# Graph network, attention layer: the product for the denominators made 96 columns wide

## The reference, cut to what matters

```python
x_l = (x @ W_l.T + b_l).reshape(n, H, C)
x_r = (x @ W_r.T + b_r).reshape(n, H, C)
z = jax.nn.leaky_relu(x_l[src] + x_r[dst], NEG_SLOPE)
e = jnp.einsum('ehc,hc->eh', z, att)
m = jax.ops.segment_max(e, dst, num_segments=n)
e = jnp.exp(e - m[dst])
denom = jax.ops.segment_sum(e, dst, num_segments=n)
alpha = e / (denom[dst] + 1e-16)
out = jax.ops.segment_sum(alpha[:, :, None] * x_l[src], dst, num_segments=n)
```

## Time and profile before

| | us |
|---|---|
| median of 3 runs | 2270.53 |
| lowest, highest | 2264.11, 2282.12 |
| the profiled execution | 2274.55 |
| its span, first to last instruction | 2272.7 |

### The profile page before, as it was taken

One profiled execution on the slowest core, in us unless ns is written; L12 is line 12 of the kernel. 1 busy time (PEld: TensorE's weight loads), 2 busy tenths in 40 slices (PEclk: granted clock), 3 DMA queues, 4 the chain that ended last, 5 costly groups with the idle time before them and its releaser, 6 DMA issues.

```text
span 2272.7 us, 38002 instructions
## 1 busy us (share of the span) xinstructions
PE 1752.6 (77%) x8603; PEld 1346.9 (59%) x8603; DVE 1805.4 (79%) x5399; ACT 1109.9 (49%) x2822; POOL 858.8 (38%) x861
## 2 busy tenths in 40 slices
PE   2677777898999998734688788778937778777886
PEld 1322224777888787523678678778925555555554
DVE  7988887899899896776877778876287787877775
ACT  0666665887888785200224324233434454444443
POOL 2000000000000000067777777771017777777771
PEclk7665557999999999766566777675557888878778
DMA  4245555765666666055656566552112222222221
GB/s 149 106 147 153 152 151 167 290 232 192 236 254 218 234 249 225 7 169 158 175 162 181 163 171 183 166 167 66 46 37 56 54 55 55 55 55 55 56 55 41
DMA packets 192476, 314.96 MB, mean 139 GB/s; under 512 B 25873, under 2 KB 139416, under 8 KB 182418
## 3 DMA queue, kind: packets, MB, share of 16 engines
q1 hardware_dynamic: 163312, 248.12, 33.4%
q0 software_dynamic: 27712, 63.56, 10.7%
q10 hardware_dynamic: 1250, 0.86, 0.1%
HBM read 232.38 MB, written 80.07 MB: 137 GB/s over the span
## 4 chain that ended last, share of the span: by engine, by line
PE 20%; POOL 17%; DVE 14%; issue 10%; DMA 3%; ACT 2%; SPq 1%; DVEq 1%; POOLq 0%; ACTq 0%
POOL G L683 12%; PE PS L1896 6%; PE PS L1872 3%; POOL G L668 3%; PE PS L2003 2%; PE PS L1897 2%; POOL SCR L668 2%; DVE HOT_R L1159 1%; PE PS L1786 1%; DVE SCR L1334 1%; DMA G<-table,src_idx 1%; DMA G<-table,gather_idx 1%; DMA SCR<-table,src_idx 1%; DVE RX L1349 1%; DVE RX L1594 1%
## 5 line engine op out<-in xcount | busy, mean ns | idle before, releaser
L668 POOL DMA_INDIRECT G<-table,src_idx x252 | 266.1, 1056 | 982.2 <-DMA table<-RX 901.9
L683 POOL DMA_INDIRECT G<-table,gather_idx x415 | 405.4, 977 | 281.0 <-DMA table<-RX 154.8
L2003 PE MATMUL PS<-SCR,OH 128*128 128x256 f32 x830 | 283.9, 507 | 107.9 <-DVE SCR L1631 106.0
L2003 PEld LDWEIGHTS PS<-SCR,OH 128*128 128x128 f32 x830 | 203.8, 255 | 161.8 <-DVE SCR L1631 119.2
L1872 PE MATMUL PS<-RX,OH 128*128 x830 | 189.4, 393 | 122.1 <-DVE SCR L1334 71.5
L1786 PE MATMUL PS<-ALL_R 128*128 128x256 f32 (+3 forms) x2025 | 266.4, 288 | 19.6 <-DVE ALL_R L1222 9.1
L1896 PE MATMUL PS<-AT 128*128 128x128 f32 x830 | 261.9, 412 | 13.5 <-DVE AT L1498 5.9
L1786 PEld LDWEIGHTS PS<-ALL_R 128*128 128x128 f32 (+1 forms) x2025 | 251.1, 190 | 22.4 <-DVE ALL_R L1222 9.5
L1872 PEld LDWEIGHTS PS<-RX,OH 128*128 128x128 f32 x830 | 160.6, 274 | 147.9 <-issue 144.6
L825 ACT ACTIVATE AT<-iota,EI 128x128 f32<-128x128 f32 x415 | 132.2, 389 | 201.2 <-PE PS L1897 201.2
L1734 PE MATMUL PS<-AT,G 128*128 128x400 bf16 x474 | 172.5, 491 | 65.7 <-DVE AT L1115 47.3
(11 more groups left out here) (395 smaller groups left out, 3377.1 us busy)
## 6 DMA issues: line engine op xcount, KB each, us to landing
ALL_R<-adjacency SPq DMA_DIRECT2D x72, 1600.0 KB, 6.8
adjacency<-ALL_R SPq DMA_DIRECT2D x26, 1600.0 KB, 7.4
AT<-gathered_rows SPq DMA_DIRECT2D x103, 256.0 KB, 3.7
gathered_rows<-G SPq DMA_DIRECT2D x63, 256.0 KB, 2.3
AT<-dst_in_block SPq DMA_DIRECT2D x103, 128.0 KB, 3.9
gathered_rows<-SCR SPq DMA_DIRECT2D x40, 256.0 KB, 2.3
G<-table,gather_idx POOLq DMA_INDIRECT x415, 2.5
G<-table,src_idx POOLq DMA_INDIRECT x252
```

The source lines that it names most:

```text
L668: pool.indirect_dma_start(score_rows(i)[:, q], None, tables[0], bass.IndirectOffsetOnAxis(ap=src_idx[:, v:v + 1], axis=0)).then_inc(s(f"sc ...
L683: pool.indirect_dma_start(G[:, p, q, :], None, tables[i], bass.IndirectOffsetOnAxis(ap=gather_idx[:, p, q:q + 1], axis=0)).then_inc(s(f"{n ...
L2003: ins = pe.matmul(PS[:, q, 0:MSG], OH[:, p, q, :], view(SCR, M_AT + (p * VB + q) * MSG, [[1, MSG]]), start=True, stop=True)
```

## The change

The 8 values of a visit (4 probabilities, 4 maxima) are copied by ACT into a place of their own, 96 columns wide, of which 88 hold zeros, and PE's second product takes all 96 columns. It therefore also adds zeros to the columns of up to 11 blocks behind its own. The place is in `means`: 2 x 4 x 96 values, two batches deep, zeroed once by DVE at the start of the stage. ACT's copy stands between the activations of line 825 and 829; ahead of it are waits for the group's probabilities and maxima, and for the sums of the batch two before. Nothing else is changed; `DENS`, `SUM_STEPS` and the order on PE and DVE stay.

```diff
+        PAD = 96
+        assert 2 * SB * PAD <= NBLK * 32 and DENS + 8 * (NBLK - 1) + PAD <= Z_PS
+
+        def padded(j):
+
+            return means, j % 2 * SB * PAD
...
                 ins.then_inc(s("sum_distance"), 1)
+                i = GROUP_OF[j]
+                act.wait_ge(s("probs_ready"), i + 1)
+                act.wait_ge(s("maxima_placed"), 2 * i + 1)
+                if j >= 2:
+                    act.wait_ge(s("sum_done"), j - 1)
+                act.copy(view(*padded(j), [[PAD, n], [HEADS, 2], [1, HEADS]]), view(HT, v * HEADS, [[HEADS, n], [MS_AT, 2], [1, HEADS]]))
                 act.wait_ge(s("sum_distance"), j + 1)
                 hot = hot.rearrange("p a b -> p (a b)")[:, 0:n * P]
                 act.activation(hot, hot, ACT.Relu, bias=1.0, scale=-1.0).then_inc(s("sum_hot"), 1)
...
+            done(dve.memset(view(means, 0, [[1, 2 * SB * PAD]]), 0.0))
             pack_words()
...
-                    ins = pe.matmul(PSF[:, bass.ds(b * 8 + DENS, 8)], OHS(j)[:, q], view(HT, (v + q) * HEADS, [[MS_AT, 2], [1, HEADS]]),
+                    ins = pe.matmul(PSF[:, bass.ds(b * 8 + DENS, PAD)], OHS(j)[:, q], view(padded(j)[0], padded(j)[1] + q * PAD, [[1, PAD]]),
                                     start=False, stop=False, skip_group_check=True)
```

## The result

The change makes the kernel faster: 2243.64 us median (2237.0 to 2244.9, 6 runs) against 2271.81 (2264.1 to 2282.2, 6 runs) for the kernel before. The ratio is 0.986, 95% interval 0.9836 to 0.9884. The profiled execution took 2243.78 us, its span is 2242.0, against 2274.55 and 2272.7. Lines of the changed kernel in the shared part move: 668 is 675, 825 is 832, 829 is 842, 1872 is 1886, 1896 and 1897 are 1910 and 1911, 1524 is 1538; the new copy is line 839.

The account below looks back on a forecast made before the run. PE's speed was taken to bound only the 109 us from last gather to 1648; 26 us in the end plus 16 before it, 42 off 2274.55, gave 2232.6, set at 2230 for the median; ends 2217 to 2243, range 2214 to 2262.

Parts of the forecast that it names:

- The bound: Attention stage: PE's speed is the kernel's time only in the 109 us from last gather (1539) to 1648.
- The 88 columns, 0 us: PE's second product of a visit: 96 columns hide beside the weight load, 0 us; upper bound 0.32 us a visit.
- The clock: PE at the attention stage's end: wider columns raise the clock from 0.50 to 1.00 in most of it.
- doesn't do what it says: Rival, 12%: PE's clock stays at 0.50, as busy time counts or zeros don't; time 2271.
- slower: Rival, 4%: PE's clock stays and the columns do not hide under the weight load; time 2320.
- ACT's copy and waits, the memset, 0 us: Attention stage: ACT's added waits are covered, 0 us; DVE's one zeroing holds up no gathers, 0.7 us if uncovered.
- A batch in the end, 2.03 us: After the last product of line 1872: ACT's 1.83 plus 0.20 for the copy, 21 batches 42.6 us.
- the 11 us of waits and pieces: Attention stage's end: last group's pieces and PE's waits around them grow from 9.3 to 11 us.
- The lead before the end, 16 us: Before the last product of line 1872: it starts 16 us earlier (8 to 22), at about 1550.
- The clock that only comes and goes: Rival, 13%: PE's high clock falls again with waits for ACT, half of the batches at 3.42 us; time 2251.
- the sum: Whole kernel: 26 us in the end plus 16 before it, 42 us off; ends 28 and 54.

Follow-up runs that it names:

- e1: The change with its copy, waits and padded place, but PE's second product only 8 columns wide; ratio 1.0009 to the kernel before.
- e4: The change with 64 columns in place of 96, nothing else; ratio 0.9907 to the kernel before.
- e9: The change with two batches of weighted sums a step from step 86 on; ratio 0.9868 to the kernel before.
- e12: The change with two batches a step from step 86 on and POOL's species conversion moved to ACT in step 18; ratio 0.9803, 2494.4 against 2539.3 us.
- e2: The change with 96 all-zero columns, without ACT's copy and its waits, output not the reference's; ratio 0.9846 to the kernel before.
- e3: The change with 32 columns in place of 96, nothing else; ratio 0.9997 to the kernel before.
- e7: The change with constant block numbers in place of PE's word load and shifts for the weighted sums, output not the reference's; ratio 0.9785, 2229.0 us.

## Why the prediction was right, and where its sizes were off

- **The bound.** PE's speed was the time from the last gather to the last sum and nowhere else: the last gather ends at 1537.7, forecast 1535 to 1540. That holds for this chip; on those of e1 to e4 and e9 to e12 the gathers wait for DVE as well.
- **The 88 columns, 0 us.** Right at both clocks: 0.85 us for a 96-wide visit at 0.50, 0.44 to 0.45 at the high clock.
- **The clock.** Right, and the rivals "doesn't do what it says" and "slower" are out. e1 (8 columns, nothing gained) and e2 (zeros alone, all gained) show that the columns do it and that zeros serve. The Trainium skill, "TensorE: Matmul & The Clock Gate", Part 1, has the clock follow how busy PE is. Read by the busy share of the profile that fails here: 92% busy goes with 0.50 in e1 and e3, 83 and 84% with 0.91 and 0.88 in the change and e4.
- **ACT's copy and waits, the memset, 0 us.** Right: e1 has them all and is no slower than before, e2 has neither copy nor waits and its batch is as long, and ACT's batch is 1.83 us with the copy, for which I had allowed 0.20 more.
- **A batch in the end, 2.03 us: off.** It is 2.23 us. I had ACT at 1.83 + 0.20 as the bound and PE at four times 0.46. In the earlier trace rows I had read the distance of two visits inside a batch; the border of a batch costs some 0.33 us more on PE itself (0.43 in the median batch: 2.23 - 4 x 0.45), and that could be seen in the trace of before at the high clock (0.82 against 0.49). At 0.50 it is not seen: 0.85 us between all visits of a run of batches in the end of before. Over 21 batches 0.20 us are 4.2; the end took 56.8 us, forecast 54, within its ends (20 to 32 less), so that the 11 us of waits and pieces came out a little shorter. e7 has no such gap at most of its borders and 51.7 us.
- **The lead before the end, 16 us: off.** It is 9.3 us, near the lower end of 8. Of these 1.3 are the earlier last gather, so PE's lag itself shrank by 7.9. It is the same gap: with it gone in e7 the lag is 10.9 us, 15.9 less than before, and the last product starts at 1547.0, forecast 1550.
- **The clock that only comes and goes.** In part: 0.91 in place of 1.00 in the end, because it falls at the two waits for the last group. The batches did not alternate.

Forecast 2230, measured 2243.6: 14 us too far, and at the slow edge of the sum's own ends (2217 to 2243); 28 us were gained where the sum has 42. The end (26 - 23.6 = 2.4) and the lead (16 - 9.3 = 6.7) make 9.1 of it; a further 2.7 is the last layer of this one profile, and the rest, 2 us, is the difference between profiled executions and medians. Cause, place and direction are as forecast; both sizes were too large, for the most part by one gap that was not counted. With it gone (e7) the lag is 15.9 us shorter and the end 28.7, together 45 against the 42 of the sum.

## What to carry to other kernels

An fp32 product with 128x128 weights cost the same start to start here with 8 columns as with 96 or 128 (0.43 us at 0.50); that it is the weight load it waits for is the likely reason, not tested. Where such narrow products keep PE busy at a clock of 0.50 and PE sets the time, try them wider, filled up with zeros, and at more than one width: 32 gave nothing here, 64 nearly all of it in the end and 0.9% against 1.5% in the whole. Size the new pace from a stretch that already runs at the high clock, and over the border of a batch, not inside it: register loads and address arithmetic on PE did not show at 0.50 here and came out when the products were twice as fast. Then ask which part of the time PE alone sets, since the higher clock was worth 24 us in the 80 at the end (0.50 to 0.91) and 9 us in the 455 before it (0.70 to 0.83).

## What the runs showed of the hardware that was not expected

**A long operation on POOL stretches one on DVE.** Behind its last gather POOL converts 3200 values a partition. The DVE operation that meets it lasts until the conversion is over. In the kernel before:

```profile
1538.35 3.96 DVE L1444 SCALAR_TENSOR_TENSOR HB<-HB,RX 32x128 f32<-32x128 f32 x2
...
1539.01 2.86 POOL L671 CAST AT<-AT 128x3200 f32<-128x3200 int32 x1
```

In e7 it meets another operation, a copy of 4 values, which otherwise takes 0.17 us:

```profile
1535.61 3.32 DVE L1470 COPY AT<-RX 128x4 f32<-128x4 f32 x1
...
1536.03 2.87 POOL L678 CAST AT<-AT 128x3200 f32<-128x3200 int32 x1
```

The Trainium skill, "SBUF — State Buffer", "Who interferes with whom", says that DVE and GpSimd share a pair of ports as an exclusive lock for a whole instruction, where DVE runs in a two-port mode or reads two operands from SBUF. The stretch agrees with a lock in that DVE's copy ends within 0.03 us of the conversion (1538.93 and 1538.90); that it starts 0.42 us before it in the profile does not fit simply, and who was first is not shown. Not every operation of DVE is held. In e9 two copies out of PSUM run beside the conversion at their usual 0.17 us, and the scan after them, which reads two operands from SBUF, takes 1.60 us where the same scan takes 0.95 in the changed kernel:

```profile
1683.96 2.87 POOL L678 CAST AT<-AT 128x3200 f32<-128x3200 int32 x1
...
1685.84 0.17 DVE L1438 COPY SCR<-PS 4x32 f32<-4x32 f32 x1
1686.04 1.60 DVE L1440 TENSOR_TENSOR_SCAN SCR<-HB,SCR 4x384 f32<-4x384 f32 x1
```

In the kernel before and in the change the stretch lies in DVE's work just where PE lags; what it costs the whole is only argued, since the conversion was taken away only together with the new schedule (e12), where it costs little.

**Chips differ.** Where the kernel before takes 2539 to 2582 us, the last gather is done at 1662 to 1710 us in place of 1539, with a single gather on POOL as long as before (1.03 us). What is added is POOL's wait for DVE's addition of the gathered rows, 168 us in e1, where it was 6.5 before. DVE in its turn stands idle at that addition with nothing in the profile to explain it for 113 us between 1110 and 1530 (24 in the kernel before, where another 40 are put down to the gathers' transfers). That the rows land later there would fit; it is not shown. The last layer, which has gathers too, is longer by about as much (153 us, and 147 up to the last gather): 778 us from the last sum to the end of the span in e1, 625 in the kernel before. The end of the attention stage, which has no gathers, is as long there: 56.0 us in e2, 56.8 with the change here, and 80.4 and 80.7 us in e1 and e3 where it was 80.4. The cause is open.
